# Second offset convolution moved behind the first deformable half, and an output read moved ahead of the second shift

## The chip, the cores and the metric

The kernel runs on one core of one Trainium2 chip. The metric is the device time of one execution in microseconds. Three executions of the kernel before are shown, and one further execution was recorded by the hardware profiler; all rows below come from that one.

## What is computed

The input `x` has the shape (8, 32, 192, 192) in float32. Two residual blocks follow one another, each on a group norm `_gn` (16 groups of 2 channels):

```python
x = x + _L0_conv_ref(_gn(x), w_off, b_off, w_dcn, b_dcn)   # shifted sampling, then 3x3 conv
x = x + _L1_conv_ref(_gn(x), w1, b1, w2, b2)               # dynamic depthwise 3x3 conv
```

The first block makes two shifts for every pixel of every channel plane with a 3x3 convolution (32 to 64 channels), takes `(sigmoid(.) - 0.5) * 2`, so that a shift is less than one pixel in x and in y, samples the plane bilinearly at the shifted place with reflection at the edges, and convolves the samples (3x3, 32 to 32). The second block averages each plane, makes 9 taps per channel with two small matrix products, and convolves each plane with its own taps.

## The kernel before, in words

One chunk is 16 image rows (4 blocks of 4 rows by 32 channels, 128 partitions), so an image has 12 chunks and the program 96. The loop runs over `STEPS` = 113 steps. In step `i` the engines work on several chunks at once: chunk `n = i` is convolved for its offsets and sampled, chunk `d = i - 3` (`DCN_STEP`) is convolved after sampling ("deformable"), and chunk `c = i - 17` (`DW_STEP`) goes through the depthwise convolution and out. Steps 0 to 16 have no depthwise work, steps 17 to 95 have everything, steps 96 to 112 have no offsets.

Each engine walks through the steps with a sequence of its own, written out by hand; the engines meet by semaphores.

- **TensorE** (`@block.tensor`, loop behind L448): `offsets(n, 0)` makes the x shifts of chunk n into the PSUM tile `z`, `offsets(n, 1)` the y shifts, each as 12 pairs of matmuls (the two of a pair are on the two column halves and run together). `deform(d, h)` and `depthwise(c, h)` are 6 pairs each, one for each half `h` of a chunk, into `dc` and `dw`. All are issued by `conv` (L333). There is one `dc` tile of two halves. `deform(d, 0)` therefore waits with `wait(pe, y_done, n)` until VectorE has read the sums of the chunk before. Once an image, `y_means`, `hidden`, `taps` and `y_bias` make the second block's means and taps, and `x_mean`, `x_var`, `x_biases` those of the next image's norm (small matmuls into `sm`).
- **ScalarE** (`@block.scalar`): `offset(n, i)` reads `z` with Tanh into `du` or `dv` (L488), `side(n, i)` makes the sign mask `mu` or `mv` from it (L495; `mirror_row`, L517, adds an edge row to `mv` in the first and last chunk of an image), `size(n, i)` makes the magnitude (L502). `sides(n + 1)` copies the next chunk's left neighbours into `nb` (L509, L510). `finish(c, h)` reads `dw` with the bias into `ot` (L523). `y_square` sums squares of finished chunks (L542), `x_sums` those of the next image's input (L531, L534).
- **VectorE** (`@block.vector`): `sample(n)` is nine instructions, L637 to L665. The first (L637) needs `mu`; the second (L644) and all behind it need `mv`. Then `evacuate(i - 3)` (L675) adds `dc`, the bias and the residual into `yr` and signals `y_done`.
- **GpSimd** sets padding columns and the per-image statistics. **SyncE** issues all loads, shifted copies and stores.

VectorE's sequence in a step is two calls:

```python
for i in range(STEPS):
    if i < TOTAL:
        sample(i)
    if 0 <= i - DCN_STEP < TOTAL:
        evacuate(i - DCN_STEP)
```

Of the kernel before, what the change touches and what calls it, by code (L numbers as in the profile page):

```python
# [21 lines left out]
TOTAL = B * CHUNKS  # L22
# [51 lines left out]
def ring(n, slots, dmas):  # L74

    return 16 * sum(dmas(m) for m in range(n % slots, n + 1, slots))


def pads_set(n):
    b, j = divmod(n, CHUNKS)  # L80
    return PADDED * b + (min(j, 2) + 1 if j < CHUNKS - 1 else PADDED)
# [16 lines left out]
def block_kernel(nc, x, planes, w_off, b_off, w_dcn, b_dcn, w1, b1, w2, b2, consts, out):  # L98
    with ExitStack() as ctx:
# [108 lines left out]
        def wait(eng, s, value):  # L208
            if value > 0:
                eng.wait_ge(s, value)  # L210
# [4 lines left out]
        def s_at(n):  # L215
            return n % SS * NB
# [110 lines left out]
        def _(pe):  # L327
            halves = (slice(0, 2 * C), slice(2 * C, P))

            def conv(acc, weights, whole, moved):  # L330
                for kx in range(3):
                    for m, view in zip(halves, (whole, moved)):
                        last = nc.tensor.matmul(acc[m], weights[:, kx, :], view[:, :, kx:kx + W],  # L333
                                                start=kx == 0, stop=kx == 2)
                return last

            def offsets(n, i):
                b, j = divmod(n, CHUNKS)
                v = xv[n % XS]
                if i == 0:  # L340
                    pe.wait_ge(x_in[n % XS], ring(n, XS, x_dmas))
                    pe.wait_ge(pads, pads_set(n))
                    if j == 0:
                        pe.wait_ge(wo_ok, b + 1)
                wait(pe, z_read, 2 * (n - 1) + i + 1)
                for h in range(2):
                    k = slice(HALF * h, HALF * h + HALF)
                    last = conv(z[:, i, h, 0:HALF * W], wos[b % 2][:, i], v[:, ABOVE, k, :], v[:, BELOW, k, :])
                last.then_inc(off_mm, 1)

            def deform(n, h):
                b, j = divmod(n, CHUNKS)
                k = s_at(n) + HALF * h
                if h == 0:
                    if j == 0:
                        pe.wait_ge(wd_ok, b + 1)
                    pe.wait_ge(s_sh[n % SS], ring(n, SS, s_dmas))
                    if j < CHUNKS - 1:
                        pe.wait_ge(s_sh[(n + 1) % SS], ring(n + 1, SS, s_dmas))
                    else:  # L360
                        pe.wait_ge(h_pads, 2 * b + 2)
                    wait(pe, y_done, n)
                acc = dc[:, HALF * h:HALF * h + HALF, 0:W]
                weights = wds[b % 2]
                if j < CHUNKS - 1 or h == 0:
                    conv(acc, weights, sr[:, k:k + HALF, :], sh[:, k:k + HALF, :]).then_inc(dcn_mm, 1)
                    return

                edge = SS * NB + b % 2
                parts = ((slice(0, C), slice(0, C), sr[:, k:k + 2, :]),  # L370
                         (slice(C, 2 * C), slice(C, 2 * C), sr[:, k:k + 2, :]),
                         (slice(2 * C, 3 * C), slice(0, C), sh[:, k:k + 2, :]),
                         (slice(3 * C, P), slice(C, 2 * C), sh[:, k:edge + 1:edge - k, :]))
                for kx in range(3):
                    for m, cols, view in parts:
                        last = nc.tensor.matmul(acc[m], weights[:, kx, cols], view[:, :, kx:kx + W],  # L376
                                                start=kx == 0, stop=kx == 2)
                last.then_inc(dcn_mm, 1)
# [71 lines left out]
            for i in range(STEPS):  # L450
                b, o = divmod(i, CHUNKS)
                c, d = i - DW_STEP, i - DCN_STEP
                if i < TOTAL:
                    offsets(i, 0)
                    offsets(i, 1)
                if 0 < b <= B and o == 4:
                    hidden(b - 1)
                if 0 < b <= B and o == 5:
                    y_bias(b - 1)
                if c >= 0:  # L460
                    depthwise(c, 0)
                if 0 <= d < TOTAL:
                    deform(d, 0)
                if 0 < b <= B and o == 4:
                    taps(b - 1)
                if c >= 0:
                    depthwise(c, 1)
                if 0 <= d < TOTAL:
                    deform(d, 1)
                if 0 < b <= B and o == 3:  # L470
                    y_means(b - 1)
                if b + 1 < B:
                    if o == 9:
                        x_mean(b + 1)
                    if o == 10:
                        x_var(b + 1)
                    if o == 11:
                        x_biases(b + 1)

        @block.scalar  # L480
        def _(act):
            def offset(n, i):
                b, j = divmod(n, CHUNKS)
                s = n % 2
                d = (du, dv)[i][s]
                act.wait_ge(off_mm, 2 * n + i + 1)
                wait(act, sampled, n - 1)
                nc.scalar.activation(d[:].rearrange("p (h k) w -> p h (k w)", h=2),  # L488
                                     z[:, i, :, 0:HALF * W], ACT.Tanh, bias=ob[b % 2][:, i:i + 1], scale=0.5)\
                    .then_inc(z_read, 1)  # L490
                act.wait_ge(z_read, 2 * n + i + 1)

            def side(n, i):
                s = n % 2
                nc.scalar.activation((mu, mv)[i][s][:], (du, dv)[i][s][:], ACT.Relu, scale=-1.0)\  # L495
                    .then_inc(prepped, 1)
                if i == 1 and n % CHUNKS in (0, CHUNKS - 1):
                    mirror_row(n)

            def size(n, i):  # L500
                d = (du, dv)[i][n % 2]
                nc.scalar.activation(d[:], d[:], ACT.Abs, scale=0.5).then_inc(prepped, 1)  # L502
# [16 lines left out]
            def finish(n, h):  # L519
                act.wait_ge(dw_mm, 2 * n + h + 1)  # L520
                if h == 0:
                    wait(act, o_out[n % 2], 16 * (n // 2))
                nc.scalar.activation(ot[n % 2][:, HALF * h:HALF * h + HALF, :], dw_bank(n, h),  # L523
                                     ACT.Identity, bias=wb[:]).then_inc(o_done, 1)
# [62 lines left out]
            for i in range(STEPS):  # L587
                b, o = divmod(i, CHUNKS)
                c, e = i - DW_STEP, i - DCN_STEP - 1
                if b + 1 < B and 0 < o <= STILES:  # L590
                    x_sums(b + 1, o - 1)
                    if o == STILES:
                        x_totals(b + 1)
                if 0 < b <= B and o == 4:
                    read("ym", b - 1, mvy[:], sm[:, C_YM:C_YM + 2])
                if 0 < b <= B and o == 5:
                    read("tap", b - 1, tapr[:], sm[:, C_TAP:C_TAP + 6])
                if b + 1 < B and o == 10:
                    read("xm", b + 1, mx[(b + 1) % 2][:], sm[:, C_XM:C_XM + 1])
                if b + 1 < B and o == 11:  # L600
                    read("xv", b + 1, vx[:], sm[:, C_XV:C_XV + 1])
                if 0 < b < B and o == 0:
                    off_bias(b)
                if i < TOTAL:
                    offset(i, 0)
                    side(i, 0)
                if 0 <= e < TOTAL:
                    y_square(e)
                if 0 < b <= B and o == 3:
                    y_totals(b - 1)  # L610
                if i < TOTAL:
                    size(i, 0)
                    offset(i, 1)
                    side(i, 1)
                    size(i, 1)
                if 0 < b <= B and o == 4:
                    read("hid", b - 1, hid[:], sm[0:HID, C_HID:C_HID + 1], ACT.Relu, bias=b1c[:], scale=1.0 / G)
                if 0 < b <= B and o == 5:
                    read("wb", b - 1, wb[:], sm[:, C_WB:C_WB + 1], bias=mvy[:, 0:1])
                    act.wait_ge(small_rd, SMALL["wb", b - 1] + 1)  # L620
                if c >= 0:
                    finish(c, 0)
                if i + 1 < TOTAL:
                    sides(i + 1)
                if c >= 0:
                    finish(c, 1)
# [300 lines left out]
```

## Time and profile before

| | us |
|---|---|
| median of 3 executions | 1674.36 (1672.02 to 1674.77) |
| profiled execution, its own time | 1668.98 |
| its span | 1667.2 |
| TensorE matmuls busy | 1557.6 (93%) |
| VectorE busy | 1341.9 (80%) |
| ScalarE busy | 1050.6 (63%) |
| mean granted TensorE clock | 0.982 of full speed |

Span is the time from the first to the last recorded instruction. Busy times are unions per engine, so that two matmuls of a pair count once. In the rows, a time in square brackets is the engine's idle time just before the instruction, with the one that ended it. PE is TensorE, DVE is VectorE, ACT is ScalarE, POOL is GpSimd.

### The profile page before, as it was taken

The numbers are of one execution on the slowest core, as the hardware profiler recorded it, in microseconds if no ns is written. First come the engines' busy times: TensorE is split into PE (matmuls) and PEld (weight loads), VectorE is DVE, ScalarE is ACT, GpSimd is POOL, SyncE is SP. The second block draws the span as 40 slices with busy tenths as digits, with TensorE's granted clock in tenths as the row PEclk, the third lists the DMA queues.
The fourth block names the chain that finished last, engine by engine and source line by source line (L and its number), as shares of the span: only waits on it lengthen the run. The fifth ranks groups of instructions, "written<-read, shape, count | busy, mean of one in ns | idle before, by whom it ended". The sixth has DMA issues, their size and how long they took to land.

```text
span 1667.2 us, 25167 instructions
## 1 busy us (share of the span) xinstructions
PE 1557.6 (93%) x9856; PEld 730.4 (44%) x9856; DVE 1341.9 (80%) x1072; ACT 1050.6 (63%) x1546; POOL 304.9 (18%) x353
## 2 busy tenths in 40 slices
PE   3778777999999999999999999999999999999989
PEld 2334333444444444444444444444444445444334
DVE  3899979898888878898888988888788988889600
ACT  4767556766777567766677666775677665565422
POOL 3000313012230130303230122301402021400010
PEclk9899989999999999999999999999999999999999
DMA  6367657667686667767586676776586775666422
GB/s 227 114 193 199 164 149 206 193 190 194 181 229 193 180 176 213 201 192 194 167 230 196 185 198 177 223 192 188 166 224 192 196 189 158 184 168 170 118 86 105
DMA packets 296631, 304.28 MB, mean 183 GB/s; under 512 B 16288, under 2 KB 263616, under 8 KB 296512
## 3 DMA queue, kind: packets, MB, share of 16 engines
q1 hardware_dynamic: 296144, 302.05, 64.8%
q8 instruction: 78, 1.28, 0.3%
q0 software_dynamic: 368, 0.61, 0.1%
q14 instruction: 41, 0.34, 0.1%
HBM read 188.96 MB, written 37.75 MB: 136 GB/s over the span
## 4 chain that ended last, share of the span: by engine, by line
PE 81%; DVE 9%; issue 3%; ACT 3%; DMA 3%; POOL 1%; SPq 1%; DVEq 0%; POOLq 0%; ACTq 0%
PE z L333 38%; PE dc L333 21%; PE dw L333 19%; DMA st<-in_planes 2%; DVE nb L656 1%; DVE nb L651 1%; DVE nb L654 1%; DVE xv L644 1%; DVE nb L658 1%; DVE nb L660 1%; PE sm L406 1%; PE dc L376 1%; DVE nb L645 1%; DMA yr<-in_planes 1%; PE sm L437 1%
## 5 line engine op out<-in xcount | busy, mean ns | idle before, releaser
L333 PE MATMUL z<-xv,wos 128*64 128x384 f32 x4608 | 772.0, 491 | 30.7 <-issue 19.6
L333 PEld LDWEIGHTS z<-xv,wos 128*64 128x64 f32 x4608 | 347.3, 137 | 427.5 <-issue 406.3
L333 PE MATMUL dc<-sr,wds 128*64 128x384 f32 x1104 | 394.7, 496 | 31.6 <-DVE yr L675 31.6
L333 PE MATMUL dc<-sh,wds 128*64 128x384 f32 x1104 | 395.1, 496 | 0.0
L333 PE MATMUL dw<-yr,wy 128*64 128x384 f32 x1008 | 356.1, 489 | 1.2 <-ACT ot L523 1.1
L333 PE MATMUL dw<-yh,wy 128*64 128x384 f32 x1008 | 356.2, 489 | 0.0
L637 DVE COPY_PREDICATED nb<-mu,xv 128x2280 f32<-128x2280 uint16 x96 | 267.7, 2788 | 101.2 <-ACT mu L495 101.2
L333 PEld LDWEIGHTS dc<-sr,wds 128*64 128x64 f32 x1104 | 152.0, 139 | 221.8 <-issue 210.1
L488 ACT ACTIVATE du<-z,ob 128x768 f32<-128x768 f32 x96 | 86.2, 898 | 250.8 <-PE z L333 250.7
L509 ACT ACTIVATE nb<-xv 128x2292 f32<-128x2292 f32 x96 | 202.5, 2110 | 40.6 <-issue 40.3
L333 PEld LDWEIGHTS dw<-yr,wy 128*64 128x64 f32 x1008 | 135.7, 137 | 166.0 <-issue 148.4
L644 DVE COPY_PREDICATED xv<-mv,xv 128x768 f32<-128x768 uint16 x96 | 100.6, 1048 | 93.5 <-ACT mv L495 70.7
L654 DVE TENSOR_TENSOR nb<-nb,du 128x1536 f32<-128x1536 f32 x96 | 169.4, 1764 | 3.3
L656 DVE TENSOR_TENSOR nb<-nb,xv 128x1536 f32<-128x1536 f32 x96 | 169.0, 1761 | 3.3
L651 DVE TENSOR_TENSOR nb<-nb,xv 128x1536 f32<-128x1536 f32 x96 | 168.8, 1758 | 3.3
L333 PEld LDWEIGHTS dc<-sh,wds 128*64 128x64 f32 x1104 | 152.0, 139 | 5.5 <-issue 1.2
L523 ACT ACTIVATE ot<-dw,wb 128x384 f32<-128x384 f32 x168 | 96.2, 572 | 79.7 <-PE dw L333 79.3
L333 PEld LDWEIGHTS dw<-yh,wy 128*64 128x64 f32 x1008 | 135.7, 137 | 3.6 <-issue 0.6
L675 DVE SCALAR_TENSOR_TENSOR yr<-dc,db,yr 128x768 f32<-128x768 f32 x96 | 97.0, 1010 | 22.8 <-PE dc L333 15.9
L542 ACT ACTIVATE junk<-yr,nmx 128x768 bf16<-128x768 f32 x96 | 88.6, 923 | 40.5 <-DVE yr L675 40.5
L531 ACT ACTIVATE st<-st,npiv 128x1152 f32<-128x1152 f32 x56 | 70.1, 1252 | 68.1 <-DMA st<-in_planes 67.9
L488 ACT ACTIVATE dv<-z,ob 128x768 f32<-128x768 f32 x96 | 86.1, 897 | 30.0 <-PE z L333 29.8
(111 smaller groups left out, 1466.4 us busy)
## 6 DMA issues: line engine op xcount, KB each, us to landing
xv<-in_x SPq DMA_DIRECT2D x272, 384.0 KB, 4.7
out<-ot SPq DMA_DIRECT2D x96, 384.0 KB, 3.4
yh<-yr SPq DMA_DIRECT2D x179, 192.0 KB, 7.7
yr<-in_x SPq DMA_DIRECT2D x88, 384.0 KB, 8.2
st<-in_planes SPq DMA_DIRECT2D x56, 576.0 KB, 7.3
sh<-sr SPq DMA_DIRECT2D x160, 194.0 KB, 2.8
sh<-sr SPq DMA_DIRECT2D x32, 145.5 KB, 2.5
yr<-in_planes SPq DMA_DIRECT2D x8, 576.0 KB, 10.7
```

The lines of the kernel that those rows point to most:

```text
L333: last = nc.tensor.matmul(acc[m], weights[:, kx, :], view[:, :, kx:kx + W], start=kx == 0, stop=kx == 2)
L488: nc.scalar.activation(d[:].rearrange("p (h k) w -> p h (k w)", h=2), z[:, i, :, 0:HALF * W], ACT.Tanh, bias=ob[b % 2][:, i:i + 1], scale= ...
L509: nc.scalar.activation(nb[s][:, :, :, 1:W], v[:, :, :, 1:W], ACT.Copy)
L523: nc.scalar.activation(ot[n % 2][:, HALF * h:HALF * h + HALF, :], dw_bank(n, h), ACT.Identity, bias=wb[:]).then_inc(o_done, 1)
L531: nc.scalar.activation(st[s][:], st[s][:], ACT.Identity, bias=npiv[:], accum_out=xs1[:, i:i + 1]).then_inc(centred, 1)
L542: nc.scalar.activation(junk[:].rearrange("p (k w) -> p k w", w=W), yr[:, k:k + NB, 1:W + 1], ACT.Square, bias=nmx[b % 2][:], accum_out=ys2 ...
L637: nc.vector.copy_predicated(q[:, :, :, 1:W - 1], m3[:, :, :, 1:W - 1], v[:, :, :, 3:W + 1]).then_inc(lerp, 1)
L644: nc.vector.copy_predicated(v[:, ABOVE, :, 1:W + 1], m1, v[:, BELOW, :, 1:W + 1]).then_inc(lerp, 1)
L651: nc.vector.tensor_tensor(two, two, own, ALU.subtract).then_inc(lerp, 1)
L654: nc.vector.tensor_tensor(two, two, u2, ALU.mult).then_inc(lerp, 1)
L656: nc.vector.tensor_tensor(two, two, own, ALU.add).then_inc(x_free, 1)
L675: nc.vector.scalar_tensor_tensor(out=y, in0=dc[:, :, 0:W], scalar=db[b % 2][:], in1=y, op0=ALU.add, op1=ALU.add, accum_out=ys1[b % 2][:, j ...
```

## The change

TensorE issues `offsets(i, 1)` behind `deform(i - 3, 0)`, no more directly behind `offsets(i, 0)`. ScalarE issues the three instructions of the y shift (`offset(i, 1)`, `side(i, 1)`, `size(i, 1)`) behind `finish(c, 0)`, no more ahead of it. No instruction is added or taken away, and no wait is changed.

```diff
@@ TensorE, one step @@
                 if i < TOTAL:
                     offsets(i, 0)
-                    offsets(i, 1)
                 if 0 < b <= B and o == 4:
                     hidden(b - 1)
...
                 if 0 <= d < TOTAL:
                     deform(d, 0)
+                if i < TOTAL:
+                    offsets(i, 1)
                 if 0 < b <= B and o == 4:
                     taps(b - 1)
@@ ScalarE, one step @@
                 if i < TOTAL:
                     size(i, 0)
-                    offset(i, 1)
-                    side(i, 1)
-                    size(i, 1)
...
                 if c >= 0:
                     finish(c, 0)
+                if i < TOTAL:
+                    offset(i, 1)
+                    side(i, 1)
+                    size(i, 1)
                 if i + 1 < TOTAL:
                     sides(i + 1)
```

**TensorE, a step in the middle of the program.** `z` is written by the offset convolutions, `dw` by the depthwise, `dc` by the deformable one; `y_done` is VectorE's signal from L675. Before:

```order
L333 MATMUL z<-xv,wos 64x384 [waits z_read,pads,x_in2]
L333 MATMUL z<-xv,wos 64x384 x11
L333 MATMUL z<-xv,wos 64x384 [waits z_read]
...
L333 MATMUL dw<-yr,wy 64x2x192 [waits o_done]
...
L333 MATMUL dc<-sr,wds 64x2x192 [waits y_done,s_sh0,s_sh2]
```

The same step now:

```order
L333 MATMUL z<-xv,wos 64x384 [waits z_read,pads,x_in2]
L333 MATMUL z<-xv,wos 64x384 x11
L333 MATMUL dw<-yr,wy 64x2x192 [waits o_done]
...
L333 MATMUL dc<-sr,wds 64x2x192 [waits y_done,s_sh0,s_sh2]
...
L333 MATMUL z<-xv,wos 64x384 [waits z_read]
L333 MATMUL z<-xv,wos 64x384 x11
```

The second group of `z` now stands behind the matmul that waits for `y_done`.

**ScalarE, a step in the middle of the program.** Before:

```order
L495 ACTIVATE mu<-du 128x768 [waits z_read]
L542 ACTIVATE junk,ys<-yr,nmx 128x768 [waits y_sq,y_done]
L502 ACTIVATE du<-du 128x768
L488 ACTIVATE dv<-z,ob 128x768 [waits sampled,off_mm]
L495 ACTIVATE mv<-dv 128x768 [waits z_read]
L502 ACTIVATE dv<-dv 128x768
L523 ACTIVATE ot<-dw,wb 128x384 [waits o_out1,dw_mm]
L509 ACTIVATE nb<-xv 128x12x191 [waits sampled,pads,x_in0]
```

Now (the line numbers are one or two higher):

```order
L496 ACTIVATE mu<-du 128x768 [waits z_read]
L543 ACTIVATE junk,ys<-yr,nmx 128x768 [waits y_sq,y_done]
L503 ACTIVATE du<-du 128x768
L524 ACTIVATE ot<-dw,wb 128x384 [waits o_out1,dw_mm]
L489 ACTIVATE dv<-z,ob 128x768 [waits sampled,off_mm]
L496 ACTIVATE mv<-dv 128x768 [waits z_read]
L503 ACTIVATE dv<-dv 128x768
L510 ACTIVATE nb<-xv 128x12x191 [waits sampled,pads,x_in0]
```

The output read of the first depthwise half stands ahead of the read of the y shifts.

## Rows read from the trace of the kernel before

**Rows 1.** The page: busy time of each engine, and the chain that ended last.

```profile
PE 1557.6 (93%) x9856; PEld 730.4 (44%) x9856; DVE 1341.9 (80%) x1072; ACT 1050.6 (63%) x1546; POOL 304.9 (18%) x353
PE 81%; DVE 9%; issue 3%; ACT 3%; DMA 3%; POOL 1%; SPq 1%; DVEq 0%; POOLq 0%; ACTq 0%
```

**Rows 2.** The chain in order of time, two steps: start us, us, what.

```profile
517.41 7.74 PE z L333 x48
525.15 1.94 PE dw L333 x12
527.09 1.94 PE dc L333 x12
...
532.89 7.74 PE z L333 x48
```

**Rows 3.** The timeline of VectorE, one step: L644 to L675 (start us, us, instruction).

```profile
706.99 1.04 DVE L644 COPY_PREDICATED xv<-mv,xv 128x768 f32<-128x768 uint16 x1 [1.00 <-ACT mv L495]
...
717.33 1.01 DVE L675 SCALAR_TENSOR_TENSOR yr<-dc,db,yr 128x768 f32<-128x768 f32 x1
```

**Rows 4.** The timeline around it: TensorE's first depthwise matmul, and ScalarE.

```profile
704.96 0.48 PE L333 MATMUL dw<-yr,wy 128*64 128x384 f32 x1
...
705.18 0.90 ACT L488 ACTIVATE dv<-z,ob 128x768 f32<-128x768 f32 x1 [0.43 <-PE z L333]
...
706.11 0.84 ACT L495 ACTIVATE mv<-dv 128x768 bf16<-128x768 f32 x1
...
711.64 1.26 ACT L531 ACTIVATE st<-st,npiv 128x1152 f32<-128x1152 f32 x1
```

**Rows 5.** The timeline of a step without depthwise work, three engines.

```profile
169.25 1.01 DVE L675 SCALAR_TENSOR_TENSOR yr<-dc,db,yr 128x768 f32<-128x768 f32 x1
...
170.31 0.94 ACT L542 ACTIVATE junk<-yr,nmx 128x768 bf16<-128x768 f32 x1 [4.96 <-DVE yr L675]
...
170.42 0.51 PE L333 MATMUL dc<-sr,wds 128*64 128x384 f32 x1 [3.02 <-DVE yr L675]
...
172.89 0.84 ACT L495 ACTIVATE mv<-dv 128x768 bf16<-128x768 f32 x1
...
173.77 1.04 DVE L644 COPY_PREDICATED xv<-mv,xv 128x768 f32<-128x768 uint16 x1 [0.78 <-ACT mv L495]
```

**Rows 6.** The timeline of TensorE behind its idle times of 3 us and more.

```profile
96.13 0.87 PE L333 MATMUL dc<-sr,wds 128*64 128x384 f32 x1 [7.72 <-DVE yr L675]
102.07 7.92 PE L333 MATMUL z<-xv,wos 128*64 128x384 f32 x48
...
125.84 0.51 PE L333 MATMUL dc<-sr,wds 128*64 128x384 f32 x1 [3.03 <-DVE yr L675]
...
228.25 10.49 PE L333 MATMUL z<-xv,wos 128*64 128x384 f32 x48 [8.36 <-issue]
...
285.17 0.27 PE L431 MATMUL sm<-pooled,w1r 128*64 128x1 f32 x1 [4.21 <-POOL pooled L794]
```

**Rows 7.** A stretch of windows: us, PE, PEld, DVE, ACT, POOL busy (count), PEclk, DMA share, GB/s.

```profile
98.00:100.00 2.00, 2.00 (x9) 0.81 (x7) 1.18 (x2) 1.97 (x3) 0.00 (x0) 0.50 0.87 236
```

**Rows 8.** The chain in order of time, behind idle times of 4.21 and 4.15 us.

```profile
285.44 3.38 PE dc L333 x12
...
1572.18 4.11 PE dc L333 x12
1576.29 2.96 PE dw L333 x12
```

**Rows 9.** The timeline of TensorE behind idle times of 2.25 us, at image borders.

```profile
810.75 7.96 PE L333 MATMUL z<-xv,wos 128*64 128x384 f32 x48 [2.25 <-issue]
1004.53 9.65 PE L333 MATMUL z<-xv,wos 128*64 128x384 f32 x48 [2.25 <-issue]
```

**Rows 10.** The chain in order of time: L644 of step 3, and ScalarE's read of the means.

```profile
84.62 1.05 DVE xv L644
...
279.44 0.07 ACT mvy L561
```

**Rows 11.** The timeline of VectorE: L644 of step 95, the last with offsets.

```profile
1560.67 1.05 DVE L644 COPY_PREDICATED xv<-mv,xv 128x768 f32<-128x768 uint16 x1 [1.46 <-ACT mv L517]
```

**Rows 12.** Waits, summed over the whole span (total us, times, longest).

```profile
PEld dw L333 <- ACT ot L523: 8.3, 18, 1.8
```

## The prediction

> **What bounds the kernel now.** I read the page first: TensorE is busy for 93% of the span and holds 81% of the chain that ended last [rows 1]. The chain in order of time says how: from one group of offset matmuls to the next are 532.89 - 517.41 = 15.48 us, and a group of 6 pairs takes 1.94 us [rows 2]. A step with all its work is 48 pairs, so 8 x 1.94 = 15.5 us: TensorE has no pause in it. Next I read what VectorE and ScalarE do beside that. VectorE's L644, which needs the mask `mv`, starts at 706.99; L675, which releases `y_done`, starts 10.34 us later and takes 1.01 [rows 3]. ScalarE starts `dv` 0.22 us after the first matmul behind the offsets, `mv` 0.93 later, and L644 follows 0.88 after that: 2.03 us in all [rows 4]. In steps without depthwise work (13 of them count below) another loop sets the pace. The end of L675 at 170.26 releases both `deform` (170.42) and ScalarE's squares (170.31), and behind these stand `dv`, `mv` and L644 at 173.77 [rows 5]: 3.51 + 11.35 = 14.86 us a step.
>
> **What the change does to the waits.** `deform(i-3, 0)` waits for `y_done` of the chunk before, which VectorE gives in step i-1, behind `sample(i-1)`. Before, `offsets(i, 1)` stood ahead of this wait, so TensorE could make the y shifts of chunk i while VectorE still sampled chunk i-1. Now they stand behind it, and VectorE cannot pass L644 of chunk i without them. This closes a loop through three engines that has one step in it:
>
> - VectorE, start of L644 to the end of L675: 10.34 + 1.01 = 11.35 [rows 3]
> - end of L675 to the first `deform` matmul: 170.42 - 170.26 = 0.16 [rows 5]
> - `deform(., 0)`, 6 pairs: 1.94, and `offsets(., 1)`, 12 pairs: 3.87 [rows 2]
> - end of the offsets to L644: 2.03 [rows 4]
>
> The sum is **19.35 us a step**. TensorE's other work is 15.48 - 5.81 = 9.67 us, and fits beside VectorE's 11.35 + 0.16 + 2.03 = 13.54; L637 (needs `mu` only) fits beside `deform` and the offsets. So 19.35 takes the place of 15.48 in full steps and of 14.86 in the early ones, and TensorE gets a pause of 19.35 - 15.48 = 3.87 us in each full step, directly ahead of `deform`, and of some 7.7 us in the early ones.
>
> **Sum at full clock.** The loop first closes from step 3 to step 4 and last from step 94 to 95. L644 of step 3 is at 84.62 and that of step 95 at 1560.67 [rows 10, 11], so these 92 steps took 1476.1 us, 16.04 each (the image borders are in it). Now:
>
> - 92 x 19.35 = 1780.2, of which 13 steps have no depthwise work and 79 have all.
> - In 15 of them `mv` gets an edge row (L517): VectorE's wait there is 1.46 against 1.00 us [rows 3, 11]. This now lies in the loop: 15 x 0.46 = 6.9.
> - Once an image `hidden` waits for the second block's means. From ScalarE's read of them at 279.44 to the matmul at 285.17 are 5.73 us [rows 6, 10]. `hidden` stands ahead of `depthwise(c, 0)` and `deform`, and 3.87 us of offsets that gave it time are gone. ScalarE reaches that read some 6.2 us after `mv` of the step before (`sides` and `finish` 3.5, sums 2.6), so `hidden` comes at 11.9, and `deform` 0.27 + 1.94 later at 14.1 against 11.5: 2.6 us, in 5 images; in the first only 0.7, because there is no depthwise work yet, and in the last with offsets nothing, because there are no sums of a next image. About 14.
> - The pauses for padding at image borders, 8.36 us once and 2.25 later [rows 6, 9], are ahead of `offsets(., 0)`, which now has 3.9 to 7.7 us to spare: they are in the old 1476.1 and cost nothing in the new sum. If that cover is gone they cost at most their old size, 8.4 + 5 x 2.3 = 20 us.
> - ScalarE's moved read: `finish(c, 0)` takes 0.57 us more ahead of `dv`. Squares, magnitude and `finish` are 1.1 + 0.8 + 0.6 = 2.5 us from `y_done`, but `dv` waits 6.0 us for the offsets: nothing. It costs 0.6 us a step at most if that cover goes. What it can give back is TensorE's wait for the output read, 8.3 us in all [rows 12], and in the new step that lies beside the pause: nothing.
> - The tail from step 96 is issued in the old order: no change.
>
> The 92 steps come to 1801 us, 325 more: a span of 1992.5.
>
> **The clock.** After idle times of 4 us and more TensorE starts at half the full clock of 2.4 GHz: behind 7.72 us idle the granted clock is 0.50, 1.2 GHz [rows 6, 7]. The two groups of `deform` behind it take 102.07 - 96.13 = 5.94 us instead of 3.88: 2.1 lost. Behind 8.36 us the offsets take 10.49 against 7.96: 2.5 [rows 6, 9]. Behind 4.21 us 6 pairs take 3.38 against 1.94: 1.4; behind 4.15 us 12 pairs take 7.07 against 3.88: 3.2 [rows 2, 6, 8]. But behind 3.03 us matmuls start at full speed (0.51), and behind 2.25 us once at no loss and once at 1.7 [rows 6, 9]. The new pause of 3.87 lies between 3.03 and 4.15; it is nearest to 4.15 and 4.21, which both lost, so I take the loss in every step. All of it falls on `deform` and `offsets(., 1)`, which are in the loop. I take the mean of the four, 9.2 / 4 = 2.3 us. The ends for a full step are 0 and 3.2. 92 x 2.3 = 212.
>
> The Trainium skill ("TensorE: Matmul & The Clock Gate", section "HAM oscillation — how this bites in real kernels") tells of a kernel in which each turn of a loop ends in a wait and the next one starts cold again, so that the price is paid in every turn. By this rule the sum has the 212; if the clock stays up in the full steps, it has only the early 13 x 2.1 = 27.
>
> Sum: 1992.5 + 212 = 2204 span; the execution is 1.8 us longer than its span, 2206, and the median is 5.4 us above the profiled time: **2211 us**. About 0.2% is what a measurement of this kernel can tell from no change.
>
> **The rivals.**
>
> 1. *The loop closes, but the clock stays up in the full steps.* For it: 3.03 us of idle did no harm once [rows 6], and TensorE runs 15.5 us without a pause in between. Against: 4.15 and 4.21. It gives 1992.5 + 27 + 7 = 2027 us. Chance 0.11.
> 2. *More than the loop.* A clock that comes back as late as at 1572 each time (3.2 us) gives 92 x 3.2 = 294, and with the 20 us of border pauses 1992.5 + 294 + 20 + 7 = 2314 us. Chance 0.08.
> 3. *TensorE stays the bound, and it is faster.* If TensorE could work on the offsets while the matmul ahead of them waits, or if VectorE's signal came in time, then the steps stay at 15.48 us and the earlier output read takes away up to the 8.3 us: 1666 us. It decides at the time from the end of L675 to L644: this must be under 15.48 - 11.35 = 4.1 us, and I count 8.0. Against it speaks that the matmuls behind a waiting one did not start in 3.03 us [rows 6]. [...] Chance 0.02.
> 4. *The change does part of this only:* the loop closes, but is shorter than I count, because VectorE's work of a chunk or a part of the mask is early. Each 1 us less is 92 us less, so it gives 1675 to 2000 us; nothing in the rows speaks for it. Chance 0.04.
>
> The order of the instructions shows the offsets behind the `y_done` wait in every step from 3 on, so that the change does nothing at all is left out.
>
> **How the numbers follow.** Forecast 0.75 (2211 us; with the loss between 1.6 and 2.7 us a step it is 2146 to 2248), rivals 0.11, 0.08, 0.02 and 0.04. The range goes from the first rival, 2025, to 2250: it holds the forecast and the first rival, 0.86, less what my sizes may be off. Faster is rival 3 alone with 0.02; within 0.2% is the near edge of rival 4, 0.01; slower is the rest, 0.97.
>
> **What would show it.** Right: steps of about 21.6 us between two L644 in the middle of the program; TensorE busy near 80% of the span with one idle time of 3.7 to 4 us in each full step, ended by L675, and a granted clock well under 0.98; VectorE's idle time ahead of L644 about 5 to 8 us in each step instead of 1; TensorE's wait for `y_done` summing to 300 to 400 us. Wrong: steps near 19.4 us with the clock at 1 (rival 1); a wait for something else ahead of `deform`, or an idle time ahead of `offsets(., 0)` in each step, would say that the loop has a member that I did not count.

## The result, and the profile after

| | before | after |
|---|---|---|
| median, us | 1673.19 | 2172.54 (2168.41 to 2174.92, 4 executions) |
| profiled execution: span | 1667.2 | 2173.1 |
| mean granted TensorE clock | 0.982 | 0.891 |

The change makes the kernel slower: the ratio is 1.298, with a 95% interval of 1.295 to 1.301, where 1.32 (2211 us) was forecast. In the tables and experiments below, "before" is always the kernel before, run on the same chip in the same session.

The page of the changed kernel, first its busy times, its chain by engine, and the two groups with the most idle time ahead of them:

```profile
PE 1728.3 (80%) x9856; PEld 823.0 (38%) x9856; DVE 1337.5 (62%) x1072; ACT 1047.5 (48%) x1546; POOL 335.7 (15%) x353
...
PE 43%; DVE 34%; ACT 11%; issue 6%; POOL 4%; DMA 1%; SPq 0%; DVEq 0%; POOLq 0%; ACTq 0%
...
L333 PE MATMUL dc<-sr,wds 128*64 128x384 f32 x1104 | 498.7, 599 | 293.0 <-DVE yr L677 293.0
...
L646 DVE COPY_PREDICATED xv<-mv,xv 128x768 f32<-128x768 uint16 x96 | 100.6, 1048 | 679.3 <-ACT mv L496 574.3
```

VectorE and ScalarE do the same work in the same time as before. TensorE's busy time is 171 us longer at the same number of matmuls, since some of them ran at half the clock. The chain was 81% TensorE [rows 1] and is now shared by three engines, which is what a loop through all of them looks like. VectorE waits 679 us ahead of L646 (L644 before), and TensorE 293 us ahead of `deform` for `yr`, a little less than the 300 to 400 us that I had expected.

The chain in order of time, one full step in the middle of the program (against the plain sequence of TensorE's groups in [rows 2]):

```profile
961.53 3.72 PE dc L333 x12
965.25 3.88 PE z L333 x24
969.16 0.91 ACT dv L489
970.09 0.85 ACT mv L496
970.97 1.05 DVE xv L646
...
981.31 1.03 DVE yr L677 x2
982.34 0.14 issue
982.47 3.49 PE dc L333 x12
```

These are the members of the predicted loop, in its order: `deform`, second offsets, `dv`, `mv`, VectorE from L646 to L677, `deform`. From one `deform` to the next are 20.94 us. Its first member takes 3.72 us, not 1.94: TensorE started at half clock (its first matmul takes 0.87 us here, 0.51 at full clock).

The timeline of VectorE, three steps of which the first took 19.40 us and the second 20.73:

```profile
1337.25 1.05 DVE L646 COPY_PREDICATED xv<-mv,xv 128x768 f32<-128x768 uint16 x1 [4.98 <-ACT mv L496]
...
1356.65 1.06 DVE L646 COPY_PREDICATED xv<-mv,xv 128x768 f32<-128x768 uint16 x1 [5.31 <-ACT mv L496]
...
1377.38 1.05 DVE L646 COPY_PREDICATED xv<-mv,xv 128x768 f32<-128x768 uint16 x1 [6.59 <-ACT mv L496]
```

The timeline of TensorE, two restarts behind the pause, 21 us apart:

```profile
940.43 0.51 PE L333 MATMUL dc<-sr,wds 128*64 128x384 f32 x1 [3.69 <-DVE yr L677]
...
961.53 0.87 PE L333 MATMUL dc<-sr,wds 128*64 128x384 f32 x1 [3.71 <-DVE yr L677]
```

The pause is the same, 3.7 us, and the first matmul behind it is at full speed once and at half speed once. Where it starts at full speed the clock can still fall right behind it (that `deform` takes 3.76 us on the chain). The trace of the kernel before had this case too, and I had not looked at it: behind 3.02 us of idle `deform` started at full speed, and from its third pair of records on it was at half speed (0.84 us for a record).

```profile
140.69 0.51 PE L333 MATMUL dc<-sr,wds 128*64 128x384 f32 x1 [3.02 <-DVE yr L675]
...
146.28 7.94 PE L333 MATMUL z<-xv,wos 128*64 128x384 f32 x48
```

Its two groups took 146.28 - 140.69 = 5.59 us instead of 3.88, so 1.7 us were lost behind a pause that I had counted among the harmless ones.

Over the 92 steps from L646 of step 3 (83.97) to that of step 95 (2069.74) the mean is 21.58 us a step.

The border of an image, from the chain in order of time (steps o = 4 and o = 5):

```profile
864.37 0.07 ACT mvy L562
...
872.63 0.26 PE sm L431
872.89 3.63 PE dw L333 x12
...
890.01 0.07 ACT tapr L562
...
895.04 0.52 PE sm L406 x12
895.55 2.94 PE dw L333 x12
```

Here GpSimd's small steps between ScalarE's read and TensorE's small matmul (8.3 us for `hidden`, 5.0 us for `y_bias`) stand ahead of `depthwise` and `deform`, and the matmuls behind them are wholly or partly at half clock (3.63 and 2.94 us for a group instead of 1.94).

### The profile page after: what moved, and what is told of

It reads as the page before. It is cut to its first block, busy times and chain, and to the rows that moved or that the text cites. A ratio compares the mean times of both kernels' runs of the same rounds, so it can differ in the third digit from the quotient of the medians.

```text
span 2173.1 us, 25167 instructions
## 1 busy us (share of the span) xinstructions
PE 1728.3 (80%) x9856; PEld 823.0 (38%) x9856; DVE 1337.5 (62%) x1072; ACT 1047.5 (48%) x1546; POOL 335.7 (15%) x353
## 4 chain that ended last, share of the span: by engine, by line
PE 43%; DVE 34%; ACT 11%; issue 6%; POOL 4%; DMA 1%; SPq 0%; DVEq 0%; POOLq 0%; ACTq 0%
PE z L333 21%; PE dc L333 17%; DVE nb L653 6%; DVE nb L658 6%; DVE nb L656 6%; PE dw L333 4%; ACT dv L489 4%; DVE xv L646 3%; DVE yr L677 3%; DVE nb L660 3%; DVE nb L662 3%; DVE nb L647 3%; ACT mv L496 3%; ACT nb L510 2%; ACT st L532 1%
## 5 line engine op out<-in xcount | busy, mean ns | idle before, releaser
L333 PE MATMUL z<-xv,wos 128*64 128x384 f32 x4608 | 829.2, 510 | 30.1 <-issue 18.8
L333 PE MATMUL dc<-sr,wds 128*64 128x384 f32 x1104 | 498.7, 599 | 293.0 <-DVE yr L677 293.0
L333 PEld LDWEIGHTS z<-xv,wos 128*64 128x64 f32 x4608 | 388.7, 145 | 447.6 <-issue 413.4
L646 DVE COPY_PREDICATED xv<-mv,xv 128x768 f32<-128x768 uint16 x96 | 100.6, 1048 | 679.3 <-ACT mv L496 574.3
L333 PE MATMUL dc<-sh,wds 128*64 128x384 f32 x1104 | 501.2, 601 | 0.0
L333 PEld LDWEIGHTS dc<-sr,wds 128*64 128x64 f32 x1104 | 174.1, 165 | 540.9 <-issue 527.5
L333 PE MATMUL dw<-yr,wy 128*64 128x384 f32 x1008 | 372.4, 507 | 1.1 <-ACT ot L524 1.1
L333 PE MATMUL dw<-yh,wy 128*64 128x384 f32 x1008 | 372.9, 508 | 0.0
L639 DVE COPY_PREDICATED nb<-mu,xv 128x2280 f32<-128x2280 uint16 x96 | 266.8, 2779 | 28.5 <-ACT mu L496 28.4
L510 ACT ACTIVATE nb<-xv 128x2292 f32<-128x2292 f32 x96 | 202.3, 2107 | 22.1 <-issue 21.8
L333 PEld LDWEIGHTS dw<-yr,wy 128*64 128x64 f32 x1008 | 140.2, 141 | 160.3 <-issue 141.3
L333 PEld LDWEIGHTS dc<-sh,wds 128*64 128x64 f32 x1104 | 174.4, 165 | 6.1 <-issue 4.0
L677 DVE SCALAR_TENSOR_TENSOR yr<-dc,db,yr 128x768 f32<-128x768 f32 x96 | 97.0, 1010 | 21.3 <-PE dc L333 14.4
L667 DVE TENSOR_TENSOR sr<-nb 128x768 f32<-128x768 f32 x96 | 92.2, 961 | 12.5
```

The lines of the kernel that those rows point to most:

```text
L510: nc.scalar.activation(nb[s][:, :, :, 1:W], v[:, :, :, 1:W], ACT.Copy)
L639: nc.vector.copy_predicated(q[:, :, :, 1:W - 1], m3[:, :, :, 1:W - 1], v[:, :, :, 3:W + 1]).then_inc(lerp, 1)
L646: nc.vector.copy_predicated(v[:, ABOVE, :, 1:W + 1], m1, v[:, BELOW, :, 1:W + 1]).then_inc(lerp, 1)
L667: nc.vector.tensor_tensor(sr[:, k:k + NB, 1:W + 1], q[:, ABOVE], q[:, MID], ALU.add)\
L677: nc.vector.scalar_tensor_tensor(out=y, in0=dc[:, :, 0:W], scalar=db[b % 2][:], in1=y, op0=ALU.add, op1=ALU.add, accum_out=ys1[b % 2][:, j ...
```

## Experiments

Times of L646 (L644 or L651 where a kernel has fewer or more lines) were read for all 96 steps of each trace. "A full step" is the mean over the 47 steps from 17 on that are not at an image border (o = 2, 3, 6 to 10). It is 15.62 us before and 21.15 after the change.

### e1: TensorE's part alone

```diff
 # against the changed kernel: ScalarE as before
+                    offset(i, 1)
+                    side(i, 1)
+                    size(i, 1)
...
                     finish(c, 0)
-                if i < TOTAL:
-                    offset(i, 1)
-                    side(i, 1)
-                    size(i, 1)
```

> TensorE's part alone: offsets(i, 1) behind deform(i-3, 0), ScalarE's old order. Theory (a loop of one step through y_done, deform, the second offsets, dv and mv, and VectorE): finish(c, 0) now comes 3.4 us after the second offsets end, which delays the second depthwise half, but that lies beside VectorE's 13.5 us; the time stays that of the change, 2160 to 2180 us, and steps at full clock stay at 19.4 us. Rival (ScalarE's moved read carries a good part of the loss, because it delays dv): faster than the change by over 50 us.

Measured: 2145 and 2200 us, two executions, with mean granted clocks of 0.895 and 0.855; the first is the one that was profiled, with a span of 2143.4. So TensorE's part makes the loss. Whether ScalarE's part adds or saves a per cent they do not tell: only the first is comparable with the 2172.5 of the change.

The steps are not what I expected. A full step took 20.57 us on the mean, none less than 20.40, and TensorE waited in another place:

```profile
976.00 0.90 PE L333 MATMUL dw<-yr,wy 128*64 128x384 f32 x1 [3.08 <-ACT ot L524]
```

In a full step there is no wait of 0.3 us or more for `y_done` left, and the chain in order of time does not pass through VectorE:

```profile
969.04 3.90 PE z L333 x24
...
972.97 0.91 ACT dv L489
...
974.65 0.83 ACT dv L503
975.47 0.48 ACT ot L524
...
976.00 3.85 PE dw L333 x12
```

With ScalarE's old order the late second offsets close a second loop, between TensorE and ScalarE: offsets, `dv`, `mv`, magnitude, output read, second depthwise half, and TensorE's own work up to the next offsets. At full clock it is 15.48 + 3.08 = 18.6 us, less than the 19.4 of the predicted loop. Measured are 20.4: the 1.8 more are clock (that half takes 3.85 us instead of 1.94), and the matmuls that are slow here lie outside VectorE's loop. The moved output read takes this second loop away. So e1 does not show the predicted loop by itself; the chain of the changed kernel, e3, e4 and e9 do.

### e2: ScalarE's part alone

```diff
 # against the kernel before
-                    offset(i, 1)
-                    side(i, 1)
-                    size(i, 1)
...
                     finish(c, 0)
+                if i < TOTAL:
+                    offset(i, 1)
+                    side(i, 1)
+                    size(i, 1)
```

> ScalarE's part alone: finish(c, 0) ahead of dv, TensorE's old order. Theory: the second offsets still stand ahead of the wait for y_done, so no loop closes. mv comes some 2.5 us later in a full step (behind the first depthwise half), VectorE ends at 8.2 us of the next step, deform starts at 9.7: 1.5 us to spare. 1665 to 1685 us. Rival (any lateness of mv costs): 79 x 2.5 us more, 1870 us.

Measured: 1706.9 us, ratio 1.019 (1.016 to 1.021). The rival, 1870 us, is out: a full step takes 15.59 us. But 20 to 40 us more than I expected are lost, at borders: step o = 1 takes 20.8 us (17.8 before), o = 4 takes 19.0 (15.9) and o = 5 takes 18.2 (17.2). A late `mv` makes VectorE end late, and what is started by its end comes late; for o = 1 this fits the wait that e7 and e10 show below, for the others it was not tried. The timeline of TensorE in a step o = 1, against 2.25 us of idle in [rows 9]:

```profile
831.25 9.66 PE L333 MATMUL z<-xv,wos 128*64 128x384 f32 x48 [4.65 <-issue]
```

### e3: the second offsets ahead of the wait

```diff
 # against the changed kernel
                     depthwise(c, 0)
+                if i < TOTAL:
+                    offsets(i, 1)
                 if 0 <= d < TOTAL:
                     deform(d, 0)
-                if i < TOTAL:
-                    offsets(i, 1)
```

> The second offsets between depthwise(c, 0) and deform(d, 0): two groups of 6 pairs earlier than in the change by only one group, but ahead of the wait for y_done. ScalarE as in the change. Theory: no loop, mv 1.9 us later than before, VectorE still has 2 us to spare: 1660 to 1685 us. Rival (the lateness of the second offsets is what costs, not the wait ahead of them): half of the loss stays, about 1900 us.

Measured: 1758.7 us, ratio 1.049 (1.047 to 1.052). `offsets(i, 1)` and `deform(d, 0)` have changed places against the changed kernel, and 414 of 499 us are back. The timeline of VectorE shows a full step of 15.48 us again, with its idle time at 1.4 us:

```profile
747.02 1.04 DVE L646 COPY_PREDICATED xv<-mv,xv 128x768 f32<-128x768 uint16 x1 [1.39 <-ACT mv L496]
...
762.50 1.05 DVE L646 COPY_PREDICATED xv<-mv,xv 128x768 f32<-128x768 uint16 x1 [1.43 <-ACT mv L496]
```

So it is the wait ahead of the second offsets that costs, and not their lateness: they come only one group earlier than in the change. My number was 75 us too low: the steps o = 4, 5 and 1 take 23.5, 19.2 and 21.0 us (15.9, 17.2 and 17.8 before). `hidden` now comes 3.87 us earlier in TensorE's sequence than before and waits for GpSimd (e7 moves it back and cures o = 4, but not o = 5).

### e4: the signal early, the order as changed

```diff
 # VectorE, against the changed kernel
                 nc.vector.copy_predicated(q[:, ABOVE], m1, q[:, BELOW]).then_inc(lerp, 1)
+                if n >= DCN_STEP:
+                    evacuate(n - DCN_STEP)
...
                 if i < TOTAL:
                     sample(i)
-                if 0 <= i - DCN_STEP < TOTAL:
+                elif i - DCN_STEP < TOTAL:
                     evacuate(i - DCN_STEP)
 # SyncE: residual(i - DCN_STEP) goes directly behind store(...);
 # s_dmas counts the third copy of an image's first chunk
```

> The change's order on both engines, but VectorE evacuates dc in the middle of sample(i), behind L647, so that y_done comes 3.1 us after the start of L646 and not 11.4 us; the residual's load is issued earlier to be there. Theory: the loop shrinks by 8.3 us to 11.1, TensorE is the bound again at 15.48 us a step: 1660 to 1690 us. Rival (VectorE's later start on mv costs by itself): over 1800 us.

Measured: 1827.5 us, ratio 1.090 (1.087 to 1.092). The place of the second offsets is that of the changed kernel, yet a full step is 15.79 us. The timeline of VectorE:

```profile
774.35 1.05 DVE L646 COPY_PREDICATED xv<-mv,xv 128x768 f32<-128x768 uint16 x1 [1.38 <-ACT mv L496]
...
776.41 1.02 DVE L679 SCALAR_TENSOR_TENSOR yr<-dc,db,yr 128x768 f32<-128x768 f32 x1
...
789.83 1.05 DVE L646 COPY_PREDICATED xv<-mv,xv 128x768 f32<-128x768 uint16 x1 [0.97 <-ACT mv L496]
```

The loop is cut at another place, and the 5.4 us a step go too: with e3 that shows the loop. The total misses my 1690 by 137 us, again at the borders (27.6, 22.7 and 21.6 us in steps o = 4, 5 and 1); why step o = 4 costs 4 us more here than in e3 was not followed up.

### e5 and e9: the pause filled

```diff
 # e5 with 8, against the changed kernel; e9 with 4, against e6
+                if 0 <= d and i < TOTAL:
+                    pe.wait_ge(z_read, 2 * i)
+                    for _ in range(8):
+                        nc.tensor.matmul(z[0:2 * C, 1, 0, 0:HALF * W], kc[:, 0:2 * C],
+                                         wo[:].rearrange("p a b c -> p (a b c)"), start=True, stop=True)
                 if 0 <= d < TOTAL:
                     deform(d, 0)
```

> The change with 8 more matmuls of 384 columns directly ahead of deform(i-3, 0) in each step from 3 to 95, on constant weights into a part of z that the second offsets overwrite: 8 x 0.32 = 2.6 us of TensorE's pause of 3.9 us is filled, the results are the same. Theory (the loop of 19.38 us at full clock plus the lost clock): in the full steps the clock stays at 2.4 GHz and steps go to 19.4 us; the change's trace has a mean step of 21.6 us, of which about 1.8 is clock: 79 x 1.8 = 140 less, 2030 us. Rival (the steps above 19.4 us are long for another reason, a transfer or ScalarE): the time does not fall, and 93 x 2.6 us of more work may lengthen it.

Measured: 2239.9 us, ratio 1.340 (1.337 to 1.343): slower than the change. The experiment was mis-sized. Its timeline shows the 8 matmuls at two records each, and records start 0.3225 us apart (3.87 / 12): 16 of them are 5.16 us of work in a pause of 3.7:

```profile
1002.19 5.00 PE L464 MATMUL z<-wo,kc 128*64 128x384 f32 x15
```

The kernel's own matmuls make two records each as well: `offsets(n, i)` issues 12 matmuls, 6 pairs, and shows 24 records. What is called 12 pairs and 6 pairs ahead of the prediction are 6 and 3 pairs of matmuls, counted by their records. The times read from the rows are not touched by this; a count of instructions was, here.

The windows view of the same stretch has TensorE busy for all of 23 us at a granted clock of 1.00:

```profile
1000.00:1023.00 23.00, 23.00 (x128) 10.83 (x125) 16.06 (x14) 10.50 (x15) 4.14 (x4) 1.00 0.43 120
```

Most full steps were 20.64 us, which is 15.48 + 5.16: TensorE's own work, and still less than the 21.15 of the change with its clock. The total is longer because in steps o = 4 and 5 (31.1 and 27.8 us) the filler stands behind the wait for the means.

> e6 (the change with the means behind deform, 2135 us) with 4 more matmuls ahead of deform(i-3, 0) in each step from 3 to 95. In e5 one such matmul showed two records of 0.32 us, so 8 of them were 5.2 us and over-filled the pause; 4 are 2.6 us of the 3.9. Theory (loop plus lost clock): the idle time left in a full step is about 1.2 us, the clock stays at 2.4 GHz, a full step takes 19.4 us, the early ones may still lose: 79 x 1.75 = 138 less, 1997 us. Rival (what a step has over 19.4 us is no matter of the clock): 2135 us or more.

Measured: 2061.0 us, ratio 1.233 (1.227 to 1.240), where e6 without the filler has 1.277 (1.272 to 1.280) and 2135.4 us. More work makes the kernel 74 us faster. The timelines of VectorE and of TensorE:

```profile
926.70 1.05 DVE L651 COPY_PREDICATED xv<-mv,xv 128x768 f32<-128x768 uint16 x1 [5.33 <-ACT mv L501]
...
946.08 1.05 DVE L651 COPY_PREDICATED xv<-mv,xv 128x768 f32<-128x768 uint16 x1 [5.32 <-ACT mv L501]
```

```profile
918.83 0.51 PE L333 MATMUL dc<-sr,wds 128*64 128x384 f32 x1 [1.16 <-DVE yr L682]
```

and the windows view of about one step, with the granted clock (1.00) ahead of the last two columns:

```profile
907.00:926.70 19.70, 18.54 (x110) 9.37 (x108) 13.77 (x12) 12.28 (x22) 1.85 (x3) 1.00 0.64 178
```

All 47 full steps take 19.4 us (mean 19.39). That is the loop with nothing else in it, and the 1.77 us that e6 has above it (21.16, at a mean granted clock of 0.91 in these steps) are clock. The total stayed 64 us above my 1997: I had counted 79 steps where the gain of 1.77 applies to 47 and part of the border steps, and the filler costs 2.2 us in step o = 5 (24.4 against 22.2) and 1.5 in step o = 0 (21.5 against 20.0).

### e6: the means behind deform, in the change

```diff
-                if 0 < b <= B and o == 4:
-                    hidden(b - 1)
-                if 0 < b <= B and o == 5:
-                    y_bias(b - 1)
...
                     deform(d, 0)
+                if 0 < b <= B and o == 4:
+                    hidden(b - 1)
+                if 0 < b <= B and o == 5:
+                    y_bias(b - 1)
                 if i < TOTAL:
                     offsets(i, 1)
```

> The change with hidden and y_bias (TensorE, once an image each) behind deform(i-3, 0) and directly ahead of the second offsets, so that depthwise(c, 0) and deform do not wait behind the means and taps. Theory: the steps o = 4 and o = 5 of an image, 25.7 and 22.7 us in the change's trace against 21.6 on the mean, lose what is over: 6 x (4.1 + 1.1) = 31 less, about 2141 us. Rival (ScalarE waits for the hidden layer in its stead): no gain.

Measured: 2135.4 us, 37 us less than the change. Step o = 4 goes from 25.5 us to 21.2, a full step's time; o = 5 only from 22.6 to 22.2. The rest comes from steps o = 1 (20.1 against 20.6) and the early ones (21.2 against 21.65); why these are shorter was not tried. So one part of my 31 us came true, and that the total is near it is partly luck.

### e7 and e10: borders, with the second offsets ahead of the wait

```diff
 # e7, against e3
-                if 0 < b <= B and o == 4:
-                    hidden(b - 1)
-                if 0 < b <= B and o == 5:
-                    y_bias(b - 1)
...
                     offsets(i, 1)
+                if 0 < b <= B and o == 4:
+                    hidden(b - 1)
+                if 0 < b <= B and o == 5:
+                    y_bias(b - 1)
 # e10, GpSimd, against e7
+                    set_pads(i + 1)
                     if b + 1 < B:
                         pivot(b + 1)
-                    set_pads(i + 1)
                     set_pads(i + 2)
```

> As e3 (second offsets ahead of the wait), with hidden and y_bias behind the second offsets, as far behind as in the kernel before. Theory: what e3 lost against before lay at the image borders alone, in the steps o = 4 (24 against 15.9 us), o = 5 (19.1 against 17.2) and o = 1 (22.1 against 17.8); the first two go: 6 x 10 = 60 of the 82 us, and 1700 us are left. Rival (they only move to another wait): over 1740 us.

Measured: 1707.3 us, ratio 1.023 (1.019 to 1.026), 7 us off. Step o = 4 is down from 23.5 to 17.1 us; o = 5 is not (20.2). There TensorE waits ahead of `depthwise(c, 0)` for the taps' weights `wy`, which GpSimd makes, and not behind `y_bias`:

```profile
902.14 0.54 PE L333 MATMUL dw<-yr,wy 128*64 128x384 f32 x1 [2.37 <-POOL wy L833]
```

Step o = 1 still has 20.3 us. The timeline of GpSimd shows why:

```profile
824.02 0.35 POOL L707 TENSOR_SCALAR npiv<-st 128x1 f32<-128x1 f32 x1 [16.41 <-DMA st<-in_planes]
824.35 5.69 POOL L759 TENSOR_SCALAR xv<-zero,mx 128x8 f32<-128x8 f32 x4
```

The padding (L759) that `offsets(., 0)` needs is queued behind a pivot (L707) that waits for a load of the next image's input. SyncE issues this load behind a wait for the end of VectorE's sampling in the step before.

> e7 (second offsets ahead of the wait, means behind them, 1707 us) with GpSimd setting the padding of chunk i+1 ahead of the pivot, so that the first offsets of step o = 1 don't wait for a load of the next image's input. Theory: the step o = 1, 21 to 22 us in e7, goes to 15.5 us: 7 x 6 = 42 less, about 1665 us. Rival (the padding waits for something else): 1700 us.

Measured: 1672.6 us, ratio 1.001 (0.998 to 1.003): level with before, 8 us above what I expected. The timeline of VectorE has the step o = 1 at 15.33 us:

```profile
417.62 1.05 DVE L646 COPY_PREDICATED xv<-mv,xv 128x768 f32<-128x768 uint16 x1 [2.62 <-ACT mv L518]
...
432.95 1.05 DVE L646 COPY_PREDICATED xv<-mv,xv 128x768 f32<-128x768 uint16 x1 [1.26 <-ACT mv L496]
```

### e8: the early signal in the kernel before

The edit is that of e4, on the kernel before.

> The kernel before, with VectorE's evacuation behind L645 in the middle of sample(i) and the residual's load issued earlier. Theory: full steps are bound by TensorE at 15.48 us and do not change; 13 early steps go from 14.86 to 14.0 us, as in e4: 10 us less, 1665 us. Rival: the evacuation in the middle delays VectorE and the loads behind it, and time is lost at the image borders as in e4 (steps o = 0 of 20 us against 17.4): 1700 us or more.

Measured: 1813.6 us, ratio 1.085 (1.083 to 1.088). The rival had the size right (1700 us or more), but the loss is not at the borders alone: a full step is 17.03 us, and a step o = 1 is 23.0. I had looked only at how early `y_done` would come, not at what the evacuation itself waits for. In the old order `mv` is early, and the second half of `deform` is not yet made when VectorE stands at it. The waits of VectorE in this kernel, summed (total us, times, longest), show it:

```profile
DVE yr L677 <- PE dc L333: 257.3, 75, 11.6
```

In e4 the late `mv` hides most of this wait: there it is 26.7 us in 20 times.

### e11 and e12: towards a faster kernel

```diff
 # both, GpSimd, against the kernel before
+                    set_pads(i + 1)
                     if b + 1 < B:
                         pivot(b + 1)
-                    set_pads(i + 1)
                     set_pads(i + 2)
 # e11 only, TensorE: y_bias behind depthwise(c, 0)
 # e11 only, ScalarE: y_square and y_totals behind size(i, 1)
```

> The kernel before with three moves: GpSimd's padding ahead of the pivot as in e10; y_bias behind depthwise(c, 0); ScalarE's squares and y totals behind size(i, 1). Theory: step o = 1 from 17.8 (19.1 twice, 20.9 in the first image) to 15.5: 22 us; step o = 5 from 17.2 to 15.7: 10 us; 13 early steps from 14.86 to VectorE's own 14.0 to 14.2: 10 us. Together 1674 - 42 = 1632 us. Rival (the waits come back at the next place): 1655 us or more.

Measured: 1674.7 us, ratio 1.001 (0.999 to 1.003): no gain, 43 us off. Step o = 1 fell to 15.8 us as expected and the early steps to 14.2, but an ordinary step rose from 15.48 to 15.83 us: ScalarE's squares now stand ahead of `finish(c, 0)`. The chain in order of time passes through them in such a step:

```profile
719.06 0.91 ACT dv L488
...
721.48 1.01 ACT junk L542 x2
722.50 0.47 ACT ot L523
...
723.01 2.16 PE dw L333 x12
```

TensorE's second depthwise half starts when the output read ends, 0.3 us later than its place in an unbroken row of matmuls (two groups of 1.94 us behind the end of `z` at 718.8). So the squares' new place is what costs the 0.35 us a step.

> The kernel before with one move: GpSimd sets the padding of chunk i+1 ahead of the pivot. Theory (from e10 and e11, where this step was cured and other moves cost what it gave): steps o = 1, 17.8 or 19.1 us in the kernel before and 20.9 in the first image, go to 15.5 and 14.9, nothing else changes: 6 x 2.3 + 2 x 1.3 + 6 = 22 us less, 1650 us. Rival (the clock or another wait takes it back at the image border): 1665 us or more.

Measured: **1651.3 us, ratio 0.987 (0.985 to 0.989)**, 1.3% faster than the kernel before, with the interval clear of no change. Its timeline of VectorE at the border where the kernel before has 17.8 us:

```profile
409.99 1.04 DVE L644 COPY_PREDICATED xv<-mv,xv 128x768 f32<-128x768 uint16 x1 [1.54 <-ACT mv L517]
...
424.94 1.05 DVE L644 COPY_PREDICATED xv<-mv,xv 128x768 f32<-128x768 uint16 x1 [0.79 <-ACT mv L495]
```

## Why the prediction was right, point by point

**The loop.** Right. It was predicted at 19.35 us from durations of the kernel before. The six full steps of the changed kernel that lost nothing to the clock take 19.4 us, and e9, with the clock kept up, has 19.39 on the mean of all 47. e3 and e4 cut the loop at two different places (the offsets ahead of the wait; the signal early) and both come back to 15.6 and 15.8 us. The pause ahead of `deform` is 3.2 to 3.8 us in the full steps, mostly 3.7, for 3.87. Rivals 3 (TensorE stays the bound) and 4 (a shorter loop) are out.

**The clock.** The mechanism was right, the size too large. I took 2.3 us a step from four restarts, two of which came after 7.7 and 8.4 us of idle time. The 47 full steps lose 21.15 - 19.39 = 1.76 us on the mean: 6 lose nothing (19.4 us), 10 lose 1.3 (20.7), 16 lose 1.6 (21.0) and 15 lose 2.6 to 2.9 (22.0 to 22.3). Only the early steps, with pauses of mostly 7 us and more, are near 2.3 (21.65 us). Over 92 steps the clock comes to 92 x 21.58 - 92 x 19.39 - 7 (edge rows, my own term, not measured apart) - 36 (borders, next point) = 159 us, where the forecast had 212. So it was 53 us too high, and the borders took part of that back. "Behind 3.03 us matmuls start at full speed" was a reading of the first matmul alone: behind the three pauses of 3.02 and 3.03 us the clock fell once. Rival 1 (the clock stays up in the full steps) was wrong at the change itself; e9 shows the kernel in which it would have been right. Rival 2 (3.2 us in each step) is out too.

**The borders.** The term for `hidden` was too small. I counted 5.73 us from ScalarE's read to the matmul. That was the first image's row; in the next six images of the same trace it was 6.2 to 7.6 us, and in the changed kernel it was 8.3 us in five images and 7.5 in one. The seven GpSimd instructions in between are the same, and they are slow where VectorE is busy:

```profile
869.83 2.72 DVE L639 COPY_PREDICATED nb<-mu,xv 128x2280 f32<-128x2280 uint16 x1
...
869.96 2.61 POOL L796 TENSOR_TENSOR pooled<-yn,ry 128x1 f32<-128x1 f32 x1
...
2112.55 0.19 POOL L796 TENSOR_TENSOR pooled<-yn,ry 128x1 f32<-128x1 f32 x1
```

L796 starts 0.13 us behind VectorE's L639 and ends with it, at 872.57 and 872.55; in the last image, with VectorE idle, it takes 0.19 us, and the time from read to matmul is 2.4 us. So the 8.3 us depend on where in VectorE's step these instructions fall. The six steps o = 4 from the second image's on were 25.5 us, 4.4 above a full step instead of 2.6. I left `y_bias` out, and 7 steps o = 5 lost 1.4 us each. Together 6 x 4.4 + 7 x 1.4 = 36 us for my 14. The padding pauses (4.33 us of idle in two steps o = 1 of the changed kernel, 2.5 in three others, 2.25 before) cost nothing on the mean, as said: such a step takes 20.6 us, less than a full one. The two with 4.33 us take 22.1, with the offsets behind the pause at half clock, and the three with 2.5 us take 19.4.

**ScalarE's moved read.** Costed at nothing, and what it does was seen too small: I had it give back at most 8.3 us of waits. Under the new TensorE order it takes away a wait of 3.08 us in each full step (e1). That is worth nothing at full clock, because the loop behind that wait is the shorter one (18.6 against 19.4). What it is worth with the clock is open: a full step of e1 is 0.6 us shorter than one of the change, from one trace each. Alone, on the kernel before, it costs 1.9% (e2), by the borders.

**The sum.** Loop 4 us low, clock 53 high, borders 22 low: 27 of the 31 us between the predicted span (2204) and the measured one (2173). The other 4 are at the start and in the tail, which is 103.4 us long instead of 106.5. So the total is closer than its two outer terms: the clock's error and the borders' cancel in part, which is luck.

## What to carry to other kernels

A piece of work moved behind a wait is moved behind everything that this wait stands for. Follow the signal back to its engine: if that engine itself needs the moved piece (one step earlier), a loop closes, and its length, the sum of single latencies, becomes the time of a step whatever the busy shares say. Look also at what follows from the pause: on TensorE the 3.7 us of waiting cost another 1.8 in clock, so that filling part of them with useless matmuls was a gain of 74 us. And look at the loop that an unmoved piece would close (e1), before calling the move of that piece worthless. Last, where an engine's queue has a wait for something far away (here the pivot's load) ahead of something urgent, swap the two: this was worth 1.3% here, more than the 8.3 us that the change could have gained by my count.

## What the runs showed of the hardware

- A pause of 3.7 us, nearly the same in each step, left the clock up in 6 of 47 full steps and made it fall in 41; a pause of 3.08 us (e1) made it fall in every full step; behind 3.02 and 3.03 us it fell once in three times (kernel before); with 0.6 to 1.3 us of pause (e9) the granted clock stayed at 1.00 in all 47. The fall can come after the matmuls have started again: the `deform` whose first matmul took 0.51 us took 3.76 us in all.
- A matmul of 384 float32 columns makes two records, 0.3225 us apart, whether a second one runs on the other column half or not: the filler used one half only and took as long per matmul (5.16 / 8 = 0.645 us) as a pair does (3.87 / 6).
- GpSimd's instructions on operands of one column took 0.19 us with VectorE idle, and up to 2.6 us beside VectorE, where they end within 0.1 us of the end of VectorE's instruction (the `hidden` chain of seven: 2.4 us in the last image, 8.3 in the middle ones). That VectorE holds them up is read from these times; no run was made for it.
